# ViT tower: generators' column sums and GpSimd's maximum moved into the QKV stage, second refinement of the roots into the first two attention steps

## What is computed

```python
h = tok(x)                                  # 32 images, 36 patches + 2 class rows = 38 rows of 256
h = h + attn(layernorm(h))                  # 16 heads of 16, q and k normalised per head, causal
h = h + ffn(layernorm(h))
# attn: q = x @ Wq.T, k = x @ Wk.T, v = x @ Wv.T; q, k = layernorm over the 16 values of a head
#       scores = q @ k.T, softmax, @ v, @ Wo.T + bo
# ffn:  xn = layernorm(x); abel = gelu(xn @ abel_w + abel_b); top 2 of 8 experts (256 -> 512 -> 256)
#       for i in range(3): moe_out = moe_out @ expm(gens[i])      # gens: 3 x 256 x 256
#       gate = sigmoid(concat(abel, moe) @ gc_w + gc_b); x + abel * (1 - gate) + moe * gate
```

## Time and profile before

| | us |
|---|---|
| device time, median of 3 runs | 363.5 |
| lowest and highest of them | 361.18, 363.83 |
| profiled execution, span | 368.5 |
| PE busy | 327.5 (89%) |
| DVE busy | 219.5 (60%) |
| ACT busy | 184.5 (50%) |
| POOL busy | 140.9 (38%) |

### The profile page before, as it was taken

How to read it: one execution, slowest core, us unless ns; L and a number is a source line. 1 busy time by engine, 2 the same in 40 slices (tenths; PEclk the granted TensorE clock), 3 DMA queues, 4 the chain that set the end, 5 groups by cost and what they waited for, 6 DMA issues and landing times.

```text
span 368.5 us, 6509 instructions
## 1 busy us (share of the span) xinstructions
PE 327.5 (89%) x1954; PEld 279.2 (76%) x1954; DVE 219.5 (60%) x590; ACT 184.5 (50%) x432; POOL 140.9 (38%) x147
## 2 busy tenths in 40 slices
PE   4699999927999999998889689999999999899695
PEld 4588655527888888876678689889998999797583
DVE  0019438799589999997878438767412322112585
ACT  1001354793689889974523476424442665451351
POOL 2001274005355456573004237777671654432000
PEclk9699999985599999999999779999999999999899
DMA  7524521124111110007731345554452466641443
GB/s 219 228 86 170 191 68 57 54 74 144 48 46 48 47 46 30 0 2 310 290 112 47 111 134 181 157 167 127 158 179 66 138 227 177 191 135 59 144 144 103
DMA packets 20400, 45.29 MB, mean 123 GB/s; under 512 B 2006, under 2 KB 13588, under 8 KB 20116
## 3 DMA queue, kind: packets, MB, share of 16 engines
q1 hardware_dynamic: 17588, 37.57, 31.0%
q0 software_dynamic: 2496, 6.82, 6.0%
q10 hardware_dynamic: 288, 0.55, 0.5%
HBM read 37.71 MB, written 7.22 MB: 122 GB/s over the span
## 4 chain that ended last, share of the span: by engine, by line
PE 76%; issue 7%; DVE 5%; DMA 5%; ACT 3%; POOL 2%; SPq 1%; POOLq 0%; DVEq 0%; ACTq 0%
PE banks L1570 12%; PE banks L1579 11%; PE banks L1512 11%; PE banks L1292 6%; PE banks L1427 5%; PE banks L1403 5%; PE banks L1330 3%; DMA qn_sb<-z_rows,gidx_sb 3%; PE banks L1658 3%; PE banks L1445 3%; PE banks L1376 3%; PE banks L1390 2%; PE banks L1483 2%; DMA patch_sb<-in_patches 2%; PE banks L1557 2%
## 5 line engine op out<-in xcount | busy, mean ns | idle before, releaser
L1570 PE MATMUL banks<-qn_sb,w_sb 128*128 128x128 f32 x416 | 54.3, 287 | 1.5 <-ACT qn_sb L668 1.0
L1570 PEld LDWEIGHTS banks<-qn_sb,w_sb 128*128 128x128 f32 x416 | 51.8, 203 | 2.0 <-ACT qn_sb L668 1.2
L1579 PE MATMUL banks<-w_sb,sq_sb 128*128 x208 | 49.0, 379 | 0.0
L668 ACT ACTIVATE qn_sb<-banks,col_sb 128x128 f32<-128x128 f32 x52 | 21.0, 455 | 48.5 <-PE banks L1557 48.5
L485 POOL DMA_INDIRECT y_rows<-pT_sb,sidx_sb x26 | 25.8, 991 | 45.4 <-DVE pT_sb L1201 44.4
L1201 DVE TENSOR_TENSOR pT_sb<-banks,p_sb 128x256 f32<-128x256 f32 x26 | 11.0, 425 | 53.8 <-PE banks L1579 51.1
L1579 PEld LDWEIGHTS banks<-w_sb,sq_sb 128*128 128x128 f32 x208 | 38.1, 190 | 4.4
L679 ACT ACTIVATE sq_sb<-banks,col_sb 128x128 f32<-128x128 f32 x104 | 32.6, 366 | 15.1 <-PE banks L1570 14.8
L1292 PE MATMUL banks<-patch_sb,wtok_sb 128*128 128x252 f32 (+1 forms) x120 | 29.1, 409 | 8.5 <-DMA wtok_sb<-in_w_tok 5.3
L479 POOL DMA_INDIRECT qn_sb<-z_rows,gidx_sb x26 | 27.9, 1072 | 22.7 <-PE banks L1557 13.7
L1292 PEld LDWEIGHTS banks<-patch_sb,wtok_sb 128*128 128x128 f32 x120 | 24.8, 226 | 11.6 <-DMA wtok_sb<-in_w_tok 5.3
(11 more groups left out here) (234 smaller groups left out, 645.6 us busy)
## 6 DMA issues: line engine op xcount, KB each, us to landing
...
```

What stands on the lines that cost most here:

```text
L1570: last = nc.tensor.matmul(bank[2 + 2 * s + c // 2][:, (c % 2) * 128:(c % 2 + 1) * 128], w1_sb[:, w0:w0 + 128], xsT_sb[:, (2 * s + k) * 128 ...
L1579: last = nc.tensor.matmul(bank[6 + s][:, 0:D], hidT_sb[:, s * HID + k * 128:s * HID + (k + 1) * 128], w2_sb[:, ds(e * 4 * D + k * D, D)], ...
```

## The change

POOL adds the bias for tiles 0 to 5 only, takes the maximum then, and comes to `norm(0)` behind it; the bias of tiles 6 to 10 follows `norm(2)`. DVE makes one `column_sums` in each of the QKV steps 0, 1 and 2, and `size_generators` in step 8. The wait for `hb_set` stands in `add_output(0)`. `newton(1, 0)` (reciprocal and square) stands in attention step 0 behind `norm_k(3)`, `newton(1, 1)` (the rest, which signals the roots) in attention step 1 ahead of `norm_k(4)`. Nothing is computed otherwise, and no transfer is added or moved in SP's queue.

```diff
--- before.py
+++ after.py
@@ -412,9 +412,14 @@
             rstd_of(6, NT, NT)
             pool.wait_ge(d_w, 32)
 
-            for t in range(NT):
+            def add_bias(t):
                 pool.tensor_tensor(hb_sb[0:T, t * D:(t + 1) * D], h_sb[0:T, t * D:(t + 1) * D], row_sb[0:T, R_BO:R_BO + D],
                                    ALU.add).then_inc(hb_set, 1)
+
+            for t in range(6):
+                add_bias(t)
+            pool.wait_ge(n_part, 1)
+            pool.partition_all_reduce(nrm_sb[:, 7:8], nrm_sb[:, 6:7], 128, bass.bass_isa.ReduceOp.max).then_inc(n_max, 1)
 
             def norm(t):
                 pool.wait_ge(rs_set, 1 if t < EARLY else 2)
@@ -446,9 +451,9 @@
             norm(0)
             norm(1)
             spread(0)
-            pool.wait_ge(n_part, 1)
-            pool.partition_all_reduce(nrm_sb[:, 7:8], nrm_sb[:, 6:7], 128, bass.bass_isa.ReduceOp.max).then_inc(n_max, 1)
             norm(2)
+            for t in range(6, NT):
+                add_bias(t)
             def powers(n, a, b):
                 pq = rr_sb[0:T, 0:2 * NT].rearrange("p (k t) -> p k t", k=2)[:, :, a:b]
                 pool.wait_ge(pq_set, n)
@@ -891,8 +896,24 @@
                                                        col_sb[r, C_GK + a:C_GK + a + 1], col_sb[r, C_BK + a:C_BK + a + 1], ALU.mult, ALU.add)
                 last.then_inc(kv_kept, 1)
 
+            def size_generators():
+                dve.wait_ge(n_max, 1)
+                link(nc.vector.tensor_scalar(nrm_sb[:, 8:9], nrm_sb[:, 7:8], 1.0 / THETA, None, ALU.mult))
+                link(nc.vector.tensor_scalar(nrmi_sb[:, 0:1], nrm_sb[:, 8:9].bitcast(i32), 23, None, ALU.logical_shift_right))
+                link(nc.vector.tensor_scalar(nrmi_sb[:, 1:2], nrmi_sb[:, 0:1], -126.0, float(SQUARINGS), ALU.add, ALU.max))
+                link(nc.vector.tensor_scalar(nrmi_sb[:, 2:3], nrmi_sb[:, 1:2], 20.0, None, ALU.min))
+                link(nc.vector.tensor_scalar(nrmi_sb[:, 3:4], nrmi_sb[:, 2:3], -1.0, 127.0, ALU.mult, ALU.add))
+                link(nc.vector.tensor_scalar(nrm_sb[:, 9:10].bitcast(i32), nrmi_sb[:, 3:4], 23, None, ALU.logical_shift_left))
+
+                link(nc.vector.tensor_scalar(nrm_sb[:, 10:11], nrm_sb[:, 8:9], EXPM_LIMIT / THETA, 3e38, ALU.is_ge, ALU.mult))
+                link(nc.vector.tensor_scalar(nrm_sb[:, 10:11], nrm_sb[:, 10:11], 1e10, None, ALU.mult))
+                link(nc.vector.tensor_tensor(nrm_sb[:, 11:12], nrm_sb[:, 10:11], nrm_sb[:, 10:11], ALU.subtract))
+                nc.vector.tensor_tensor(nrm_sb[:, 12:13], nrm_sb[:, 9:10], nrm_sb[:, 11:12], ALU.add).then_inc(scale_set, 1)
+
             for t in range(EARLY):
                 qkv_step(t, t % 2)
+                if t < G:
+                    column_sums(t)
             variance(0)
             for t in range(EARLY, NT):
                 qkv_step(t, t % 2)
@@ -901,15 +922,11 @@
                 elif t in (6, 7):
                     norm_k(t - 6, t - 6)
                 elif t == 8:
-                    column_sums(0)
+                    size_generators()
                 elif t == 9:
                     keep_k(0, 0)
             variance(1)
-            column_sums(1)
-            column_sums(2)
-
-
-            dve.wait_ge(hb_set, NT)
+
 
             def shift(t, s):
                 if behind(t, 2):
@@ -925,6 +942,8 @@
 
             def add_output(t):
                 dve.wait_ge(wo_made, t + 1)
+                if isinstance(t, int) and t == 0:
+                    dve.wait_ge(hb_set, NT)
                 nc.vector.tensor_tensor(h1_sb[0:T, ds(t * D, D)], bank[3][0:T, 0:D], hb_sb[0:T, ds(t * D, D)],
                                         ALU.add).then_inc(h1_added_c1, 1)
 
@@ -958,8 +977,12 @@
                     shift(t + 1, 1 - s)
                 if behind(t, 2):
                     finish(t - 2)
+                if isinstance(t, int) and t == 1:
+                    newton(1, 1)
                 if ahead(t, 3):
                     norm_k(t + 3, 1 - s)
+                if isinstance(t, int) and t == 0:
+                    newton(1, 0)
                 if isinstance(t, int) and t == NT - 1:
                     norm_z(0)
                     norm_z(1)
@@ -977,20 +1000,6 @@
                 nc.vector.scalar_tensor_tensor(out=R[1][:, a:b], in0=R[0][:, a:b], scalar=EPS, in1=mv3[:, a:b, 1], op0=ALU.mult,
                                                op1=ALU.add).then_inc(pq_set, 1)
 
-            def size_generators():
-                dve.wait_ge(n_max, 1)
...
             def norm_z(t):
                 if t in (0,) + CUT:
                     dve.wait_ge(rstd2, 1 if t == 0 else 2 + CUT.index(t))
@@ -1000,9 +1009,6 @@
             shift(0, 0)
             norm_k(2, 0)
             keep_k(1, 1)
-            newton(1, 0)
-            newton(1, 1)
-            size_generators()
             attn_tiles(dve, attn_step)
```

10 lines of the change are left out of this document (removed).

## The result

The changed kernel takes 376.18 us (median of 4 runs, 371.65 to 380.14), the kernel before 363.66 beside it (4 runs, 361.18 to 366.71). The ratio is 1.0332, 95% interval 1.0255 to 1.0408: slower by 12.5 us, far above the forecast of 363.0 and above its range. The profiled execution has a span of 374.2 and its run was timed at 376.7, 2.5 above the span; so the 368.5 of the profile before was that of a long execution (it had low clock from 12.5 to 19.4 and from 207.1 to 217.3 too), and I took another of the same kernel (label `before_again`, with the experiments): span 362.4, run 364.35. It is the one that the changed kernel's rows are compared with.

The account below looks back on a forecast made before the run. PE bounds all but the QKV-to-attention hand-over, where POOL's maximum stops it 7.28 us and its clock falls. Hand-over -2.1 plus maximum +2.3 gave +0.2 (-4.0 at high clock); -0.5 was taken: 363.0 us, range 358.5 to 367.2.

Parts of the forecast that it names:

- The term of +2.3 for the maximum: QKV stage, POOL: 6.93 us of issue on each side of the maximum delays `norm(0)` and PE's `turn_q(0)`, +2.3 us.
- rival C: QKV stage: the new stop before `turn_q(0)` already lowers PE's clock there, costing 1.7 to 3.4; 367.2 us, chance 0.17.
- the turns of tile 4 then wait for `norm(4)`: 0.4: Attention step 1: tile 4's turns wait 0.4 us for POOL's `norm(4)`, which starts together with DVE's `norm_k(4)`.
- the sum at the low clock: Whole change, clock low as long as before: -2.1 at the hand-over and +2.3 for the maximum, +0.2 us.
- rival D: Attention step 1: roots hold `norm(4)`, moving the stop there (4 us); low-clock steps cost 2 to 5 each; 365-367, chance 0.05.
- The hand-over's -2.1: QKV to attention, DVE from the end of `keep_k(1)` to `keep_k(4)`: 2.1 us less than 26.3 at the low clock.
- The other waits: Hand-over at the low clock: DVE waits for PE's `turn_k(2)`, the end of `values(0)`, and tile 3's turns; 1.4 and 1.6 for the latter two.
- the 0.7 that I had allowed for a shorter low stretch: Hand-over: a shorter stay at the low clock was thought possible, so -0.5 us was taken instead of +0.2.
- three column sums and the power of two at 0: DVE in the QKV steps: sums of 0.68 us each and 1.2 more in step 8 fit into idle time, cost 0.
- the wait for the bias and the biases' move at 0: The wait in `add_output(0)` comes 30 us after its biases; biases of tiles 6 to 10 use empty POOL time: 0.
- three operations of the roots at 1.6 without a neighbour: DVE, attention step 1: the last three root operations take 1.6 us with POOL waiting, against 3.9 when crowded.
- the sum made from it: QKV stage: with the skill's load figure on both sides of the maximum, `norm(0)` starts at 61.6, a loss of 0.4 us.

## Why the prediction was wrong

**The term of +2.3 for the maximum was mis-sized, and this is the first step that failed.** I priced each switch at 6.93, the only one that the trace showed. They took 9.01 and 9.16 (9.57 and 9.34, 9.11 and 9.21 in two other kernels): `norm(0)` came 25.7 behind the first product, not 21.3. The 4.4 more went to PE nearly one for one: its stop was 6.49 for 2.3. The clock fell 3.2 us into that stop, at 62.4, which the term did not hold; the half rate that followed cost 0.8 on the turn at 65.64 and 1.0 on the product behind it, 1.8. 2.3 + 4.4 + 1.8 is 8.5, measured were 7.9. The bound ahead of the maximum, 0 to 10.96, held the 9.01; the value taken from the nearest row didn't, and for the switch behind it I had given no bound at all, one row being all I had. The part of rival C in the QKV stage (0.17) is what came, but its price of 1.7 to 3.4 was for the clock alone; most of the 7.9 was wait. (Two slips of the text: its own terms give 2.2 for the 2.3, and 0.2 + 3.4 is 3.6 for C, not 3.7. And in the first profile the clock is low in slices 2, 11, 23 and 24 too, not only in 9 and 10. None of them changes the outcome.)

**The term "the turns of tile 4 then wait for `norm(4)`: 0.4" was mis-sized, and this is the second.** DVE waited 2.54, PE stood 3.30, and the clock fell again, to 120.4. The 0.4 was worked out for full clock and carried into the sum at the low clock unchanged. From the roots' end at 105.91 POOL's product took 2.26 and the two turns at half rate until 111.76, 5.9 together, while DVE had 3.5 of its own to do. I had the stop of 4 in rival D and gave it 0.05, reasoning that DVE is the bound there and a stop of PE costs nothing; but the same stop had to be asked what it does to the clock: step 2 took 11.08, 3.65 more, within the 2 to 5 a step of rival D's own sentence. How much of that comes is the execution's clock: 0.0 to 3.65 in the kernels with the roots in step 1. By the medians the roots' place is worth 5 to 6 us.

**The hand-over's -2.1** did not come: 26.1 against the 26.3 of the earlier trace rows. In step 1 the forecast had 7.42 - 0.9 + 1.6 + 0.2 + 0.4 = 8.7, the trace has 11.76. Of the 3.0 between them 2.1 are the wait (2.54 for 0.4) and 1.0 is DVE's row at 107.13, 1.19 for 0.21 beside POOL's `norm(4)`, a price that the forecast had for `norm_k(4)` only. The other waits were right: 2.99, 1.13 and 1.48, forecast 2.6, 1.4 and 1.6. The forecast also took the length of the low stretch for given, while it decides the part up to `keep_k(4)` more than the old stop does (the table above). Taken with the 0.7 that I had allowed for a shorter low stretch, the account between the two spans is closed: -0.5 + 5.6 (QKV stage, 7.9 for 2.3) + 2.8 + 0.7 + 3.65 - 1.4 = 10.85, and 10.8 was measured.

**Right:** three column sums and the power of two at 0; the wait for the bias and the biases' move at 0 (POOL's second group, 69.80 to 73.25, held nobody); three operations of the roots at 1.6 without a neighbour (104.33 to 105.91, 1.58); the turn of q for tile 2 behind ACT and the turn of k 2.7 behind that. The Trainium skill's figure for the load at the first call on GpSimd (GPSIMD Engine Reference, section 2.1, 5.95) is below every switch measured but two, 5.50 and 5.78, both ahead of the operation, and the sum made from it was further off than mine. It says that this load has no visible instruction; the runs agree, and show such a stand on both sides of the operation.

**How much is clock.** Over 68 timed runs of the kernel before (those beside the experiments and `before_again`), 2 x (1 - mean granted clock) x span gives the time at the low level, and a line through them gives 353.1 + 0.39 of that time, with a scatter of 1.2. The changed kernel's runs have 43 us of low level against 29 (medians), worth 5.5, and lie 6.7 above the line: by this line, which holds for a kernel other than its own only as an estimate, about half of the 12.5 is clock, half waiting at any clock. The kernel with the roots early has 26 us of it (median) and lies 1.9 below the line.

**Open:** why a switch took 9.0 to 10.6 between 45 and 66 us of the span and 5.5 to 7.3 from 63 us on, and why the one ahead of the maximum took at most 7.1 when POOL came to it at 42 us. The DMA share in the stretches (0.17 and 0.18 in most of them) doesn't order the groups, and no experiment was made on it. Open too: what makes the low stretch at the hand-over end after 14 us in one execution and after 27 in another.
